# Scoring two heads at once on half the array's rows, a later first value piece, and a bias moved to VectorE

## What is computed

```python
# layers 2 and 3: 16 heads of 64; layer 3 has biases
q = norm(x) @ Wq; k = ctx @ Wk; v = ctx @ Wv          # (B, 112, 1024), (B, 375, 1024)
out = softmax(q_h @ k_h.T / 8) @ v_h                  # per head h
x = x + concat(out) @ Wo
# layer 1
qp = relu(norm(x) @ Wq + bq); kp = relu(ctx @ Wk + bk); vp = relu(ctx @ Wv + bv)
x = x + relu((relu(qp @ kp.T) / 16 + mask) @ vp)
```

## Time and profile before

| | |
|---|---|
| median of three runs | 3923.49 us |
| profiled execution | 3921.66 us, its span 3919.8 us |
| busy in the span | PE 83%, PEld 71%, DVE 41%, ACT 40%, POOL 32% |
| wide attention of layer 2 / layer 3 | about 1797 to 2510 us / 2838 to 3577 us (heads), start-up ahead of each |
| relu attention | about 915 to 1105 us |

### The profile page before, as it was taken

One profiled execution on the slowest core, in us unless ns is written; L12 is line 12 of the kernel. 1 busy time (PEld: TensorE's weight loads), 2 busy tenths in 40 slices (PEclk: granted clock), 3 DMA queues, 4 the chain that ended last, 5 costly groups with the idle time before them and its releaser, 6 DMA issues. The chain is left out here.

```text
span 3919.8 us, 67890 instructions
## 1 busy us (share of the span) xinstructions
PE 3269.5 (83%) x22398; PEld 2797.8 (71%) x22398; DVE 1619.4 (41%) x3595; ACT 1577.4 (40%) x4385; POOL 1254.9 (32%) x1350
## 2 busy tenths in 40 slices
PE   3899829985978838938999999759599999997998
PEld 2777718873656625627888888748488888886998
DVE  2777720002246530024445444310344444444776
ACT  1555504431235522204555555324255555553222
POOL 0000030002000030034666666510266666664211
PEclk8999959997989958979999999879799999997999
DMA  6555418872100014330000000059300000000101
GB/s 176 129 130 130 97 54 317 310 258 64 35 16 0 0 35 139 113 94 13 9 12 8 8 8 5 3 199 314 115 9 8 8 8 8 8 5 6 33 25 32
DMA packets 155097, 287.81 MB, mean 73 GB/s; under 512 B 53210, under 2 KB 126748, under 8 KB 137116
## 3 DMA queue, kind: packets, MB, share of 16 engines
q1 hardware_dynamic: 147292, 267.81, 22.3%
q0 software_dynamic: 7680, 18.36, 1.8%
HBM read 240.75 MB, written 45.35 MB: 73 GB/s over the span
## 5 line engine op out<-in xcount | busy, mean ns | idle before, releaser
L712 POOL TENSOR_SCALAR L_probs<-L_probs,L_inverse 112x375 f32<-112x375 f32 x512 | 645.2, 1260 | 88.3 <-issue 88.3
L835 DVE TENSOR_REDUCE L_negmax<-bank 112x1 f32<-112x375 f32 x768 | 416.8, 543 | 406.8 <-PE bank L482 337.5
L676 ACT ACTIVATE L_probs<-bank,L_negmax 112x375 f32<-112x375 f32 x768 | 439.5, 572 | 334.0 <-DVE L_negmax L835 332.0
L710 POOL TENSOR_TENSOR L_inverse<-L_sums,neg_one 112x1 f32<-112x1 f32 x512 | 315.2, 616 | 324.1 <-ACT L_probs L676 318.5
L507 PE MATMUL bank<-ident,L_probs 112*125 112x112 f32 x2304 | 372.3, 270 | 10.4 <-POOL L_probs L712 8.6
L507 PEld LDWEIGHTS bank<-ident,L_probs 112*125 112x125 f32 x2304 | 360.1, 189 | 18.6 <-POOL L_probs L712 15.5
L657 ACT ACTIVATE L_probsT<-bank 125x336 f32<-125x336 f32 x512 | 231.3, 452 | 291.4 <-PE bank L507 289.3
L522 PE MATMUL bank<-L_probsT,v 125*64 125x112 f32 x3072 | 206.1, 270 | 1.1 <-ACT L_probsT L657 1.1
L639 ACT ACTIVATE v<-bank 125x512 f32<-125x512 f32 x192 | 114.9, 598 | 197.4 <-PE bank L432 197.4
L478 PE MATMUL bank<-L_keys_hi,L_q_hh 128*112 128x376 f32 x512 | 183.3, 358 | 0.0
L522 PEld LDWEIGHTS bank<-L_probsT,v 125*64 125x64 f32 x3072 | 150.6, 137 | 29.1 <-ACT L_probsT L657 1.6
(11 more groups left out here) (294 smaller groups left out, 7297.3 us busy)
## 6 DMA issues: line engine op xcount, KB each, us to landing
L0t_w<-in_F_w SPq DMA_DIRECT2D x70, 1024.0 KB, 5.1
L2t_w<-in_F_w SPq DMA_DIRECT2D x42, 1024.0 KB, 5.1
L_keys<-spread_k SPq DMA_DIRECT2D x64, 376.0 KB, 6.6
L_ctxT<-in_ctxT SPq DMA_DIRECT2D x48, 375.0 KB, 3.4
L1t_w<-in_F_w SPq DMA_DIRECT2D x16, 1024.0 KB, 6.0
slots_in<-zeros SPq DMA_DIRECT2D x4, 1792.0 KB, 16.5
L_q<-spread_q SPq DMA_DIRECT2D x128, 56.0 KB, 2.2
spread_k<-L_k_hi SPq DMA_DIRECT2D x16, 376.0 KB, 2.5
```

Source lines behind the costliest of these rows:

```text
L676: act.activation(probs[h % NB][:, :], psS[h % 2][0:T, 0:S], ACT.Exp, bias=negmax[b.par][:, h:h + 1], accum_out=sums[b.par][:, h:h + 1]).th ...
L710: pool.tensor_tensor(inverse[b.par][:, h:h + 1], sums[b.par][:, h:h + 1], core.neg_one[0:T, :], ALU.pow)
L712: pool.tensor_scalar(probs[h % NB][:, :], probs[h % NB][:, :], inverse[b.par][:, h:h + 1], None, ALU.mult)\
L835: dve.tensor_reduce(negmax[b.par][:, h:h + 1], psS[h % 2][0:T, 0:S], AX, ALU.max, negate=True).then_inc(maxed.sem, 1)
```

## The change

Wide attention: q_hh and q_ll become q_high and q_low without the zero halves; at even h the scores of heads h and h+1 are made together, six matmuls on 64 rows each, alternating between row halves and between the two score banks; they wait for the exponential of head h - 1. DVE and ACT do both heads' maxima and exponentials at even steps. The query split is one instruction each instead of two. POOL's zeroing and its semaphore go. In `order`, V0 moves from step 3 to 4, V1 from 4 to 5, K4 from 5 to 3.

Relu attention: bv is loaded into all 125 rows; the one-row matmul goes; DVE adds bv on the way out of the bank into vb, counted by `biased`; ACT applies the relu from vb. PE waits for `biased` before it writes a value bank again.

```diff
-        order = {0: ["K0", "K1"], 1: ["K2"], 2: ["K3"], 3: ["L0", "L1", "V0"], 4: ["V1"], 5: ["K4"], 6: ["Y0"],
+        order = {0: ["K0", "K1"], 1: ["K2"], 2: ["K3"], 3: ["L0", "L1", "K4"], 4: ["V0"], 5: ["V1"], 6: ["Y0"],
...
-            q_hh = [sb(f"q_hh{i}", [P, H, T], F32R) for i in range(2)]
-            q_ll = [sb(f"q_ll{i}", [P, H, T], F32R) for i in range(2)]
+            q_high = [sb(f"q_high{i}", [P, EC, T], F32R) for i in range(2)]
+            q_low = [sb(f"q_low{i}", [P, EC, T], F32R) for i in range(2)]
...
                 def scores(b, h):
                     if wide:
+                        if h % 2 == 1:
+                            return
...
-                        pe.wait_ge(exped.sem, exped.at(H * b.n + h - 1))
-                        pe.matmul(psS[h % 2][0:T, 0:SP], q_hh[b.par][:, h, :], keys_hi[b.par][:, c, :],
-                                  start=True, stop=False)
...
+                        pe.wait_ge(exped.sem, exped.at(H * b.n + h))
+                        for n, (qt, kt) in enumerate(((q_high, keys_hi), (q_high, keys_lo), (q_low, keys_hi))):
+                            for i in range(2):
+                                rows = slice(i * dh, (i + 1) * dh)
+                                ins = pe.matmul(psS[i][0:T, 0:SP], qt[b.par][rows, c, :], kt[b.par][rows, c, :],
+                                                start=(n == 0), stop=(n == 2))
+                                if n == 2:
+                                    ins.then_inc(scored.sem, 1)
...
-                        act.wait_ge(maxed.sem, maxed.at(H * b.n + h + 1))
-                        act.activation(probs[h % NB][:, :], psS[h % 2][0:T, 0:S],
...
+                        for e in ((h, h + 1) if h % 2 == 0 else ()) if wide else (h,):
+                            act.wait_ge(maxed.sem, maxed.at(H * b.n + e + 1))
+                            act.activation(probs[e % NB][:, :], psS[e % 2][0:T, 0:S],
...
-                    for i in range(2):
-                        rows = slice(i * dh, (i + 1) * dh)
-                        dve.tensor_copy(q_hh[b.par][rows, 8 * m + i:8 * m + 8:2, :], q[rows, :, :])
+                    dve.tensor_copy(q_high[b.par][:, 4 * m:4 * m + 4, :], q[:, :, :])
...
                     for h in range(H):
-                        head_max(b, h)
+                        for e in ((h, h + 1) if h % 2 == 0 else ()) if wide else (h,):
+                            head_max(b, e)
...
+                    if dst is bv:
+                        s = s.rearrange("a d -> (a d)").partition_broadcast(SJ)
...
-                    pe.wait_ge(taken["V"].sem, taken["V"].at(J * b.n + (j - 1)))
+                    pe.wait_ge(biased.sem, biased.at(J * b.n + (j - 1)))
...
-                    pe.matmul(psV[(b.par * J + j) % 2][0:SJ, 0:D], core.ones[0:1, 0:SJ], bv[0:1, :],
-                              start=False, stop=True).then_inc(made["V"].sem, 1)
...
-                    act.wait_ge(made["V"].sem, made["V"].at(J * b.n + (j + 1)))
-                    act.activation(v[b.par][:, j, :], psV[(b.par * J + j) % 2][0:SJ, 0:D], ACT.Relu)\
-                        .then_inc(taken["V"].sem, 1)
+                    act.wait_ge(biased.sem, biased.at(J * b.n + (j + 1)))
+                    act.activation(v[b.par][:, j, :], vb[j][:, :], ACT.Relu).then_inc(taken["V"].sem, 1)
...
+                def bias_values(b, j):
+
+                    dve.wait_ge(made["V"].sem, made["V"].at(J * b.n + (j + 1)))
+
+                    dve.wait_ge(taken["V"].sem, taken["V"].at(J * b.n + (j - 2)))
+                    dve.tensor_tensor(vb[j][:, :], psV[(b.par * J + j) % 2][0:SJ, 0:D], bv[:, :], ALU.add)\
+                        .then_inc(biased.sem, 1)
```

More of the change, by code:

```diff
@@ L472, in scores @@
                             pe.wait_ge(q_split.sem, q_split.at(NQ * b.n + h // 8 + 1))
-                        if h % 2 == 0:
-                            pe.wait_ge(taken["K"].sem, taken["K"].at(EC * b.n + (c + 1)))
-                        pe.wait_ge(exped.sem, exped.at(H * b.n + h - 1))
-                        pe.matmul(psS[h % 2][0:T, 0:SP], q_hh[b.par][:, h, :], keys_hi[b.par][:, c, :],
-                                  start=True, stop=False)
[L480 to L483, removed]
+                        pe.wait_ge(taken["K"].sem, taken["K"].at(EC * b.n + (c + 1)))
+                        pe.wait_ge(exped.sem, exped.at(H * b.n + h))
[6 more added lines that the diff above has]
+                                    ins.then_inc(scored.sem, 1)
                         return
@@ L601, in _ @@
                 pe.wait_ge(weights.sem, weights.at(16 * nweights))
-                if wide:
-                    pe.wait_ge(q_zeroed.sem, q_zeroed.at(1))
                 if mask:
@@ L721, in _ @@
                 if wide:
-                    for part in q_hh + q_ll:
-                        for i in range(2):
-                            ins = pool.memset(part[i * dh:(i + 1) * dh, 1 - i::2, :].bitcast(F32), 0.0)
-                    ins.then_inc(q_zeroed.sem, 1)
-                    pool.drain()
                     run(heads, rstd, None, lambda b: None, pool)
@@ L1757, in relu_attention @@
         v = [sb(f"v{i}", [SJ, J, D]) for i in range(2)]
+        vb = [sb(f"vb{i}", [SJ, D]) for i in range(3)]
         weightsT = sb("weightsT", [SJ, J, T])
@@ L1767, in relu_attention @@
         taken = {c: core.counter(f"taken_{c}") for c in "LQKVY"}
+        biased = core.counter("rope_done")
         loads = [(wq, w["wq"]), (wk, w["wk"]), (wv, w["wv"]), (bq, w["bq"]), (bk, w["bk"]), (bv, w["bv"]),
@@ L1841, in values @@
                 def values(b, j):
-                    pe.wait_ge(taken["V"].sem, taken["V"].at(J * b.n + (j - 1)))
+                    pe.wait_ge(biased.sem, biased.at(J * b.n + (j - 1)))
                     for k in range(DC):
-                        pe.matmul(psV[(b.par * J + j) % 2][0:SJ, 0:D], ctxT[b.par][:, k, j * SJ:(j + 1) * SJ],
-                                  wv[:, k, :], start=(k == 0), stop=False)
-                    pe.matmul(psV[(b.par * J + j) % 2][0:SJ, 0:D], core.ones[0:1, 0:SJ], bv[0:1, :],
-                              start=False, stop=True).then_inc(made["V"].sem, 1)
+                        ins = pe.matmul(psV[(b.par * J + j) % 2][0:SJ, 0:D], ctxT[b.par][:, k, j * SJ:(j + 1) * SJ],
+                                        wv[:, k, :], start=(k == 0), stop=(k == DC - 1))
+                    ins.then_inc(made["V"].sem, 1)
                 def first(b):
@@ L1943, in first @@
                     normalise_end(b)
+                    for j in range(J):
+                        bias_values(b, j)
                 def heads(b, last):
@@ L1956, in heads @@
                         .then_inc(mixed.sem, 1)
+                    if not last:
+                        for j in range(J):
+                            bias_values(b + 1, j)
                     dve.wait_ge(made["Y"].sem, made["Y"].at(b.n + 1))
@@ L1970, in relu_attention @@
             s.stage_over(B)
-        for s, n in ((made["K"], DC), (taken["K"], DC), (made["V"], J), (taken["V"], J)):
+        for s, n in ((made["K"], DC), (taken["K"], DC), (made["V"], J), (taken["V"], J), (biased, J)):
             s.stage_over(B * n)
```

19 lines of the change are left out of this document (7 added, 12 removed).

## The result

| | changed kernel | kernel before |
|---|---|---|
| median | 3815.64 us (3808.83 to 3824.66) | 3923.62 us (3920.95 to 3924.15) |
| ratio | 0.9726, 95% interval 0.9707 to 0.9745 | |
| profiled execution | 3808.83 us, span 3807.0 | 3921.66 us, span 3919.8 |

The account below looks back on a forecast made before the run. PE, 98% busy in the relu and wide attentions, was taken as the bound. The terms -37.3 - 36 - 30.4 + 12 - 3.5 = -95.2 us, from 3921.66 us, gave 3826 us; range 3790 to 3866.

Parts of the forecast that it names:

- Part 1: Relu attention: moving the values' bias from one-row PE matmuls to a DVE add gains 37.3 us, bounds 30 and 41.
- the broadcast: Relu attention's start: loading the bias row as a 125 KB broadcast among the gating loads costs 0.5 us.
- Part 2: Wide attentions: two heads' scores on half the rows each, 0.93 us a pair, gain 36 us; bounds -132 and +84.
- Rival (a): Wide score pairs: the six loads queue, 1.07 us a pair, 3 us gained instead of 36: 3859 us; chance 0.20.
- Rival (c): Wide score pairs: no charge for the array's shape, 0.52 us a pair, 132 us gained: 3730 us; chance 0.08.
- Rival (d): Wide score pairs: row halves don't run side by side, 1.45 us a pair, 84 us lost: 3946 us; chance 0.09.
- Rival (b): Wide attentions: paired exponentials hold back banks and next scores 1 us a batch beyond the charge, 30 us: 3856; chance 0.14.
- Rival (e): Relu attention: the DVE add and its two waits keep V on the path, 37 us stay: 3863 us; chance 0.04.
- Part 3: Wide attentions: V0 a step later removes PE's whole 30.4 us wait for ACT's copy of the turned input.
- Part 4: Wide attentions: pairing heads' maxima and exponentials adds waits, charged 12 us over 30 batches; bounds 0 and 30.
- the hand sum: Wide batches, engine orders followed: K2 0.3 us late, step 5 0.3 in L3, step 13 0.1.
- Part 5: Wide attentions: one query split over 128 rows saves 3.5 us at stage starts; in steady batches DVE has room.

## Why the prediction was right, and which terms were off

**Part 1, the relu bias: right.** Forecast 37.3 us, the run alone 36.5 (35 by the traces). Batches of 8.93 us for the 8.8 forecast, V calls 0.87 apart for 0.86. The one wrong term is the broadcast, 0.5 us forecast and 3 measured; that the mask's load stands behind it was read from the earlier trace rows, and its size was not worked out from anything.

**Part 2, the row halves: right, in part by luck.** Rows behave as columns do. The pair was forecast at 0.93 us: entry 0.12, 0.71 from the first load to the turn, next uncovered load 0.10. Measured: 0.09, 0.70, and 0.10 (turn to the next V piece 0.25 us before, 2894.81 to 2895.06, and 0.35 after, 2855.77 to 2856.12), 0.89 in all. Added up between starts over the steady batches of L2, a batch's scores take 8.64 us in the kernel before, 8.25 with pairs of whole rows and 5.59 with halves. Of the 2.66 that the halves take off, 0.36 come back on V, 0.35 on K where the shape is entered, and 0.80 on the eight turns behind the pairs (0.10 each), where the uncovered loads show. That leaves 1.15 us a batch, 34 us in 30, for the 1.2 and 36 forecast. One step was wrong: the four heads behind Q and Y were counted as gone at 0.59 us, but the 0.07 to 0.08 us by which each of them is dearer than the others stays, for a turn now stands in their place (Q to the next start 1.79 us instead of 1.72). These 0.3 us a batch and the 0.04 that each pair was priced too high cancel by chance. Rival (a), loads in a line, falls with the row of PEld: two in 0.17 us. On one load the trace agrees with the Trainium skill's page "TensorE: Matmul & The Clock Gate", section "LDWEIGHTS (loading the stationary operand)": the number of rows doesn't count, 0.17 us for 112 columns on 64 rows and on 128. But two loads on different rows take that only once. Rival (c), a pair in 0.52 us, was off by the price of the shape: 0.09 entering, 0.09 more in the first round, 0.10 behind the last and 0.10 behind the turn. Rival (d) is refuted by the run on the same rows. Rival (b) asked for 42 us of waits from the pairing; even on whole rows it costs 18. Rival (e) is refuted by the relu part's run alone.

**Part 3, V0's move: right place, mis-sized.** Forecast 30.4 us, alone 39.6. The step that failed is "the whole 30.4 us goes", as the size of the stop: the group of waits in the earlier trace rows counts idle from the modelled end of a 0.41 us bar, though its successor could start after 0.19. Its own instance, turn at 2891.31 and V0 at 2892.80, shows 1.30 where 1.08 is listed. It also took for granted that the parts add; behind the pairing the move is worth only 15.

**Part 4, the pairing's waits: right to charge, in other places.** Forecast 12 us. On whole rows it costs 18, and of the hand sum only the wait at step 13 is there, at 0.44 us instead of 0.1. In the changed kernel that wait is down to 0.06 us (turn to values 0.48), the K2 wait on L_keys_lo is not in the steady batches (the 3.0 us on it lie in the two stage starts), and what the pairing still costs, 8 us as the remainder of the sum below, is nearly all in the stages' first and last batches. DVE's timelines around step 13 say why the wait shrank, pairs of whole rows first, then the changed kernel:

```profile
2020.96 1.06 DVE L839 TENSOR_REDUCE L_negmax<-bank 112x1 f32<-112x375 f32 x2 [1.45 <-PE bank L485]
2022.12 1.25 DVE L832 TENSOR_TENSOR L_q_ll<-L_q,L_q_hh 64x448 fp32r<-64x448 f32 x2
2023.56 0.62 DVE L858 COPY L_oT<-bank 128x448 f32<-128x448 f32 x1 [0.18 <-issue]
```

```profile
2000.23 1.00 DVE L826 TENSOR_REDUCE L_negmax<-bank 112x1 f32<-112x375 f32 x2 [2.22 <-PE bank L481]
2001.32 0.62 DVE L819 TENSOR_TENSOR L_q_low<-L_q,L_q_high 128x448 fp32r<-128x448 f32 x1
2002.13 0.62 DVE L845 COPY L_oT<-bank 128x448 f32<-128x448 f32 x1 [0.18 <-issue]
```

Between the two maxima and the output copy stands the query's low part: two instructions on 64 rows with the old split, one with the new. The copy begins 1.97 us behind the Q piece's start (2021.59) there and 1.59 here (2000.54). So, as far as the timelines show, it is the query split and not the row halves that ends this wait; the run on the same rows, whose pairs take 1.21 us but whose split is the new one, has no such wait either. No run changed the split alone.

**Part 5, the query split: undersized, and wrong in the steady batches.** At the stage starts: in L3 the wait of the earlier trace rows went from 2.55 us to 0.54, but from the first turn of the stage to V0 it is 20.23 us before (2809.63 to 2829.86) and 17.15 after (2733.72 to 2750.87): 3.1 us, not 1.8; in L2 it is 2.2 (18.40 to 16.23). That is 5 for 3.5. "In steady batches DVE has room" is true of its busy time and was wrong for the wait at step 13: behind the pairing the second instruction costs PE 0.38 us in each batch, 11 us in 30. Together, 34 for the halves, 5 at the starts and 11 at step 13 are the 50 of the runs. PE's windows at the start of L3 in the kernel before show what else went:

```profile
2818.40:2821.00 2.60, 0.06 (x1) 0.00 (x0) 2.40 (x6) 0.58 (x1) 0.00 (x0) 1.00 0.00 0
2821.00:2824.50 3.50, 3.49 (x12) 3.49 (x13) 1.08 (x2) 0.57 (x1) 0.00 (x0) 0.56 0.00 0
```

Behind 2.6 idle microseconds the granted clock was 0.56, near the lower of its two levels (1.2 and 2.4 GHz), for 3.5 us of full work. All four traces with the old split have such a stretch at the start of L3, behind waits of 2.2 to 2.6 us; none of the nine with the new split has one, with 0.5 to 0.7 us of wait there.

**The sum.** Part 1: 37 forecast, 36.5 measured. Part 3: 30 and 40. Parts 2, 4 and 5 together: 27.5 forecast (36 - 12 + 3.5), 31 measured behind the new order (50 - 19; by stage lengths 1486.9 - 1456.2), which is 34 for the halves and 5 for the stage starts, less 8 for the pairing. So -95 against -107.5. Most of the difference is the stop in part 3: 7 us for the 0.22 us that each reading was short, and 3 not traced. The last batches of the wide stages, which follow POOL, were rightly left out: the turns' waits for POOL's weighing rose from 8.6 to 11.3 us over both stages. No sign was wrong, the mechanisms of all parts but the steady half of the query split held, and 3816 lies in the range.

## What to carry to other kernels

Read a stop as the distance between two starts, minus what the same pair of instructions needs where nothing waits; the idle column behind a short matmul of modelled length leaves part of it out. Before adding up the gains of two edits, ask if both shorten one wait: here pairing and reordering each cure the same one, the move is worth 40 us alone and 15 behind the pairing. An engine that is half idle can still keep a copy waiting behind its own queue: room in the busy time says nothing about the place in the order. A one-row matmul for a bias costs far more than its columns on an engine that sets the pace; if another engine passes over the data with room to spare, the bias belongs there, and its broadcast belongs behind the loads that gate the stage. Where the engine doesn't set the pace, freed time can go into longer waits, and in the first layer the granted clock fell behind them too.

## What the runs showed of the hardware

- Matmuls on different row halves are not held to the order of the program. With three of one half ahead of three of the other, they still ran in three couples, 0.71 us in all. The Trainium skill's page "TensorE: Matmul & The Clock Gate", section "The mechanism", says that matmuls start and end strictly in program order and only loads are pulled ahead. By that it would have been five rounds and some 83 us more; the run took none of it, so here the measurement decides. The two orders did reach the chip as different programs: the second matmul of a pair begins 10 ns (median of 256) behind the first there, and 3 ns in the changed kernel. Whether the halves run on separately or are rearranged on the way to the array no run shows.
- On the same rows the second of two loads adds 0.10 us to the first's 0.17, on other rows nothing.
- The granted clock fell to its lower level for 3.4 us behind waits of PE: seven times in the first layer without its one-row matmuls, where the wait for the turned input had grown from 0.39 to 0.73 us, and never in that stretch of the other twelve traces.
- The shape costs 0.09 to 0.10 us at each of four places around a pair. The Trainium skill, "TensorEngine Tiling (Array Packing)", section "Key Properties", says that changing the mode drains the engine and gives no price; the trace shows these four places and their length, not what happens in them.
